# A recurrent step in which r, n and z of each half of the outputs become products of their own, in another order

## The chip, the cores and the metric

One core of one Trainium2 chip runs the whole program in one launch. The metric is device time in microseconds (us), the median of several runs. TensorE (PE; its weight loads are shown apart as PEld), VectorE (DVE), ScalarE (ACT), GpSimd (POOL) and the DMA queue of SyncE (SP) run side by side and meet at semaphores.

## The reference, cut to what matters

Four residual layers over x (4 batches, 512 time steps, 512 features): an attention layer, a recurrent cell (GRU), and two short convolutions over time. The change is in the recurrent cell alone. It goes through 512 steps, each of which needs the state of the one before:

```python
def cell(h, x):
    gi = x @ W_ih + b_ih
    gh = h @ W_hh + b_hh
    i_r, i_z, i_n = jnp.split(gi, 3, axis=-1)
    h_r, h_z, h_n = jnp.split(gh, 3, axis=-1)
    r = jax.nn.sigmoid(i_r + h_r)
    z = jax.nn.sigmoid(i_z + h_z)
    n = jnp.tanh(i_n + r * h_n)
    h_new = (1.0 - z) * n + z * h
    return (h_new, h_new)
```

## The kernel before, in words

The attention layer takes the first 570 us. After it comes the recurrent part, which is nearly three quarters of the time, with the convolutions on GpSimd beside it.

**The state.** h (4 batches, 512 features) lies transposed: features on the partitions, in four blocks k of 128; `h_of` picks a half (two of the four blocks). A step makes h new half by half. Half 0 is blocks 0 and 1, half 1 is blocks 2 and 3 (the columns of W_hh are regrouped so that each half is 64 of the 128 columns of every group G). So the products over k = 0, 1 need half 0 of h, and those over k = 2, 3 need half 1.

**TensorE.** h is the stationary operand (128 partitions by 4 columns) and W_hh streams past it. One `products` call makes, for two blocks k, four products with one column group G of the array each, so that 4 of them stand side by side. Everything is float32, and the profile shows two LDWEIGHTS and two MATMULs for each product. `begin` (line 1248) does the r and n columns together (128 columns wide) for both halves of the outputs with the first half of h; `end` (line 1258) then does r and n of output half 0 with the second half of h, z of output half 0 (64 columns wide, all four k), r and n of output half 1, and z of output half 1. Between `end` and the next `begin` a `part` (line 1286) is put in the first 448 steps: a piece of the input products (x @ W_ih) of later steps, some 0.3 us of TensorE work. The last 64 steps have none. The loop over the first 448 steps is a hardware loop whose body is four steps long, the loop over the last 64 has a body of two.

**ScalarE.** It first writes the input side (`seed_rn`, `seed_z`) into the PSUM banks, onto which the products are then added. In a step it does: sigmoid of r (`reset`, line 1199), the seeding of r and n for the next step (line 1174), sigmoid of z (`update`, line 1205), tanh (`new`, line 1210), for half 0 and then for half 1; then the two z seeds (line 1178) and the copy of the input side of n (`bring`, line 1171).

**VectorE.** It works in strict order. `turn_rn` transposes r and n of a half from PSUM (two instructions of line 1069), `turn_z` does z (line 1075), `scan_n` forms i_n + r * h_n as a scan (line 1082), `scan_h` forms the new h of the half as a scan (line 1087) and releases TensorE with `s_h`. Its order in a step is turn_rn(0), turn_z(0), scan_n(0), turn_rn(1), scan_h(0), turn_z(1), scan_n(1), scan_h(1), and the sum into the output sequence (line 1100). In some steps one of `seed_n`, `take_rz` and `take_n` follows, which carry the results of `part` out of PSUM or prepare a bank for them.

An instruction that waits for two semaphores is built as a waiting instruction of its own for one of them, with the other held on the instruction itself.

## Time and profile before

| | us |
|---|---|
| median of 3 runs | 2117.09 (2116.19 to 2117.44) |
| span of the profiled execution | 2113.7 |
| what the median has over that span | 3.4 |
| attention and set-up, up to the first recurrent product | 572.4 |
| TensorE busy | 2071.9 (98%) |
| VectorE busy | 1354.9 (64%) |
| ScalarE busy | 1239.1 (59%) |
| GpSimd busy | 638.0 (30%) |

The times list no time of its own for the profiled execution; it is its span of 2113.7 us and the 3.4 us that lie around it. Busy time of TensorE is a union of overlapping matmuls whose ends are modelled, so 98% does not say that TensorE decides the length of a step. The granted TensorE clock is full in nearly every slice. What one step is made of is read from the timeline: the order of start times on the three engines, with the durations and the idle times that it prints.

### The profile page before, as it was taken

The page shows a single profiled execution, that of the slowest core. Times are in us where ns is not written, and L with a number is a line of the kernel's source. Part 1 is how long each engine was busy: PE and PEld are TensorE (multiplying, and loading weights), DVE is VectorE, ACT ScalarE, POOL GpSimd, SP SyncE. Part 2 cuts the span into 40 slices and gives each one's busy share as a digit, 9 for nine tenths or more (in the row PEclk, how much of TensorE's full clock was granted, in tenths as well). Part 3 has the DMA queues.
Part 4 walks back from the last instruction along what each step waited for, and adds up shares of the span by engine and source line. Part 5 has one row for each costly group of instructions (what it writes and reads, how often), then busy time and mean ns, then how long its engine had stood idle before and what let it go on. Part 6 is the DMA issues. An engine that isn't in the chain of part 4 may idle for free.

```text
span 2113.7 us, 181503 instructions
## 1 busy us (share of the span) xinstructions
PE 2071.9 (98%) x77848; PEld 1578.9 (75%) x77848; DVE 1354.9 (64%) x6162; ACT 1239.1 (59%) x5995; POOL 638.0 (30%) x1015
## 2 busy tenths in 40 slices
PE   8999999999999999999999999999999999999998
PEld 2222222222499999999999999999999999998887
DVE  4344445444367777777777777777777777776676
ACT  3445544443266666666666666666666666666665
POOL 0355547444112222222222222222222222222222
PEclk9999999999999999999999999999999999999999
DMA  6000000011222222221222222222121212210001
GB/s 259 1 1 1 1 1 1 1 60 31 49 54 53 52 55 52 52 55 49 69 59 55 52 53 53 56 58 66 50 58 50 58 48 60 67 30 11 5 8 20
DMA packets 218082, 96.04 MB, mean 45 GB/s; under 512 B 170216, under 2 KB 213480, under 8 KB 217320
## 3 DMA queue, kind: packets, MB, share of 16 engines
q1 hardware_dynamic: 217032, 92.00, 16.8%
q10 hardware_dynamic: 928, 2.65, 0.3%
q8 instruction: 47, 0.77, 0.2%
q14 instruction: 75, 0.61, 0.1%
HBM read 26.30 MB, written 12.58 MB: 18 GB/s over the span
## 4 chain that ended last, share of the span: by engine, by line
PE 70%; DVE 2%; issue 0%; DMA 0%; ACT 0%; SPq 0%; DVEq 0%
PE ps L1241 64%; PE ps L1274 4%; PE ps L1282 2%; DVE arena L1069 1%; DVE arena L1087 0%; DMA arena<-arena 0%; DVE arena L965 0%; DVE arena L1075 0%; DVE arena L1082 0%; DVE arena L968 0%; ACT arena L1210 0%; SPq L994 0%; DVE arena L1158 0%; DVE seq L1163 0%; DVE seq L1100 0%
## 5 line engine op out<-in xcount | busy, mean ns | idle before, releaser
L1241 PE MATMUL ps<-whh,arena 128*4 128x128 f32 (+1 forms) x65568 | 1451.4, 246 | 13.8 <-issue 1.6
L1241 PEld LDWEIGHTS ps<-whh,arena 128*4 128x4 f32 x65568 | 1293.6, 87 | 112.2 <-DVE arena L1087 25.8
L1069 DVE STREAM_TRANSPOSE arena<-ps 128x64 f32<-128x64 f32 x2048 | 446.4, 284 | 256.1 <-PE ps L1241 237.0
L1199 ACT ACTIVATE arena<-arena 128x8 f32<-128x8 f32 x1024 | 216.1, 211 | 543.4 <-DVE arena L1069 480.1
L455 DVE TENSOR_REDUCE top<-ps 128x2 f32<-128x1024 f32 x128 | 150.8, 1220 | 244.0 <-PE ps L722 244.0
L1174 ACT ACTIVATE ps<-arena 128x128 f32<-128x128 f32 x1026 | 288.9, 282 | 0.5 <-PEq L212 0.4
L1087 DVE TENSOR_TENSOR_SCAN arena<-arena 128x24 f32<-128x24 f32 x1024 | 192.1, 188 | 145.1 <-ACT arena L1210 145.1
L1075 DVE STREAM_TRANSPOSE arena<-ps 128x64 f32<-128x64 f32 x1024 | 257.5, 251 | 9.0 <-PE ps L1241 3.3
L361 ACT ACTIVATE arena<-ps 128x1024 f32<-128x1024 f32 x128 | 124.1, 1021 | 212.7 <-PE ps L798 212.6
L610 PE MATMUL ps<-arena 128*32 128x512 f32 x2048 | 242.7, 595 | 2.7 <-ACT arena L383 2.7
L965 POOL TENSOR_TENSOR arena<-tap,arena 128x128 f32<-128x128 f32 x252 | 102.0, 415 | 430.0 <-DVE seq L1100 430.0
L1210 ACT ACTIVATE arena<-arena 128x16 f32<-128x16 f32 x1024 | 222.4, 217 | 2.0 <-DVE arena L1082 2.0
L1205 ACT ACTIVATE arena<-arena 128x8 f32<-128x8 f32 x1024 | 218.9, 214 | 3.5 <-DVE arena L1075 3.2
L1082 DVE TENSOR_TENSOR_SCAN arena<-arena 128x16 f32<-128x16 f32 x1024 | 196.3, 192 | 2.3 <-DVE arena L1075 2.2
L968 POOL TENSOR_TENSOR arena<-arena 128x128 f32<-128x128 f32 x252 | 112.6, 457 | 261.5 <-DVE seq L1100 261.5
L1178 ACT ACTIVATE ps<-arena 128x64 f32<-128x64 f32 x1026 | 181.9, 209 | 0.1
L610 PEld LDWEIGHTS ps<-arena 128*32 128x32 f32 x2048 | 61.4, 110 | 158.6 <-issue 156.9
L965 POOL TENSOR_TENSOR arena<-tap,seq 128x128 f32<-128x128 f32 x252 | 101.9, 415 | 203.2 <-DVE seq L1100 203.2
L1274 PE MATMUL ps<-arena 128*32 128x114 f32 (+1 forms) x4480 | 150.4, 242 | 2.0 <-DMA arena<-arena 2.0
L273 POOL TENSOR_TENSOR arena<-arena 128x2048 f32<-128x2048 f32 x16 | 72.8, 4551 | 212.3 <-ACT arena L361 212.3
L1100 DVE TENSOR_TENSOR seq<-seq,arena 128x16 f32<-128x16 f32 x512 | 98.5, 192 | 17.8
L1171 ACT ACTIVATE arena<-arena 128x16 f32 (+1 forms) x513 | 109.8, 214 | 0.0
(99 smaller groups left out, 1268.0 us busy)
## 6 DMA issues: line engine op xcount, KB each, us to landing
arena<-arena SPq DMA_DIRECT2D x216, 114.0 KB, 2.2
arena<-arena SPq DMA_DIRECT2D x112, 128.0 KB
arena<-seq SPq DMA_DIRECT2D x224, 55.0 KB
arena<-gi_d SPq DMA_DIRECT2D x248, 32.0 KB
gi_d<-arena SPq DMA_DIRECT2D x96, 57.0 KB
out<-seq SPq DMA_DIRECT2D x14, 256.0 KB
seq<-in_x SPq DMA_DIRECT2D x3, 1024.0 KB, 15.6
whh<-in_w_hh SPq DMA_DIRECT2D x1, 3072.0 KB, 21.1
```

The lines of the kernel that those rows point to most:

```text
L610: last = e.matmul(dst[rows], w[:, rows], v, start=start, stop=stop)
L965: return e.tensor_tensor(conv_part(k, held), along(tap[:, k]), src[:, :, bass.ds(t + k, NB)], ALU.mult)
L1069: e.transpose(trn[:, h, q].rearrange("p (i c s) -> p c i s", c=2, s=2)[:, :, :, 0], bank[RN[h]][:, 64 * q:64 * q + 64].rearrange("p (c i) ...
L1075: e.transpose(trz[:, h].rearrange("p (i c) -> p c i", c=2), bank[RZ[h]][:, 0:64].rearrange("p (c i) -> p c i", c=2)).then_inc(st["s_tr"], 1)
L1082: e.tensor_tensor_scan(pre[:, h], r_d0[:, h], trn[:, h, 1, 0:2 * NH], 0.0, ALU.mult, ALU.add).then_inc(st["s_pre"], 1)
L1087: e.tensor_tensor_scan(hb[:, 1 - u, h, 0:HS], z_d0[:, h], hb[:, u, h, 1:HS + 1], 0.0, ALU.mult, ALU.add).then_inc(st["s_h"], 1)
L1174: e.activation(bank[RN[h]][:, 0:P].rearrange("p (q n) -> p q n", q=2), at(19456 + SLOT * s + 64 * h, 512).rearrange("p (q w) -> p q w", q= ...
L1199: e.activation(r_d0[:, h].rearrange("p (i s) -> p i s", s=2)[:, :, 1], trn[:, h, 0, 0:2 * NH].rearrange("p (i s) -> p i s", s=2)[:, :, 0], ...
L1205: e.activation(z_d0[:, h].rearrange("p (i s) -> p i s", s=3)[:, :, 2], trz[:, h, 0:NH], ACT.Sigmoid)
L1210: e.activation(hb[:, u, h, 1:HS + 1].rearrange("p (i s) -> p i s", s=3)[:, :, 0:3:2], pre[:, h].rearrange("p (i s) -> p i s", s=2)[:, :, 1 ...
L1241: last = e.matmul(bank[dst[h]][32 * G:32 * G + B, 0:n], hv, wv[:, k, gates, G, 64 * h:64 * h + 64], start=False, stop=k2 == 1 and k == C - ...
L1274: last = e.matmul(bank[FA][rows, columns], a_fixed[:, k, rows], a_moving[:, k, columns], start=k == 0, stop=k == C - 1, skip_group_check=True)
```

## The change

Each of r, n and z of each half gets its own region in PSUM and, but for one case, its own products (64 columns wide). r1 and z0 lie side by side in one bank and are made together, 128 columns wide, in `begin`. There is a semaphore for every completed piece, VectorE transposes every piece by itself, and the order of all three engines is rewritten. `scan_h` now waits for the sigmoid of z by a semaphore of its own (`s_zs`) beside that of tanh. The instructions that serve `part` (`gate_op`) go from the end of VectorE's step to a place ahead of `scan_h(1)`.

```diff
-        RN, RZ, FA, FN = (0, 1), (2, 3), 4, 5
+        FA, FN = 4, 5
+        gate_r = (bank[0][:, 0:64], bank[1][:, 0:64])
+        gate_n = (bank[6][:, 0:64], bank[2][:, 0:64])
+        gate_z = (bank[1][:, 64:128], bank[3][:, 0:64])
...
                     def scan_n(h):
-                        e.wait_ge(st["s_tr"], n_at[h])
                         e.wait_ge(st["s_sig"], half[h])
+                        e.wait_ge(st["s_tn"], half[h])
...
                     def scan_h(h):
+                        e.wait_ge(st["s_zs"], half[h])
                         e.wait_ge(st["s_tanh"], half[h])
...
-                    turn_rn(0)
+                    turn_r(0)
+                    turn_n(0)
+                    scan_n(0)
                     turn_z(0)
-                    scan_n(0)
-                    turn_rn(1)
+                    turn_r(1)
+                    turn_n(1)
                     scan_h(0)
+                    scan_n(1)
                     turn_z(1)
-                    scan_n(1)
+                    gate_op()
                     scan_h(1)
...
                         reset(0)
-                        e.wait_ge(st["s_tr"], turned[1])
-                        seed_rn(0, s)
+                        seed_r(0, s)
+                        new(0)
                         update(0)
-                        new(0)
                         reset(1)
-                        e.wait_ge(st["s_tr"], turned[4])
-                        seed_rn(1, s)
+                        e.wait_ge(st["s_tn"], half[0])
+                        seed_n(0, s)
+                        seed_z(0, s)
+                        seed_r(1, s)
+                        new(1)
                         update(1)
-                        new(1)
-                        seed_z(0, s)
+                        bring(following)
+                        e.wait_ge(st["s_tn"], half[1])
+                        seed_n(1, s)
                         seed_z(1, s)
-                        bring(following)
...
                     e.wait_ge(st["s_h"], half[0])
-                    e.wait_ge(st["s_seed_rn"], half[0])
-                    products(u, RN, rn, 0, 0)
-                    e.wait_ge(st["s_seed_rn"], half[1])
-                    products(u, RN, rn, 1, 0)
+                    e.wait_ge(st["s_seed_r"], half[0])
+                    products(u, gate_r[0], "r0", 0, False)
+                    e.wait_ge(st["s_seed_n"], half[0])
+                    products(u, gate_n[0], "n0", 0, False)
+                    e.wait_ge(st["s_seed_r"], half[1])
+                    e.wait_ge(st["s_seed_z"], half[0])
+                    products(u, bank[1][:, 0:128], "r1 z0", 0, False)
...
                     e.wait_ge(st["s_h"], half[1])
-                    products(u, RN, rn, 0, 1).then_inc(st["s_rn"], 1)
-                    e.wait_ge(st["s_seed_z"], half[0])
-                    products(u, RZ, z, 0, 0)
-                    products(u, RZ, z, 0, 1).then_inc(st["s_z"], 1)
-                    products(u, RN, rn, 1, 1).then_inc(st["s_rn"], 1)
+                    products(u, gate_r[0], "r0", 1, True).then_inc(st["s_r0"], 1)
+                    products(u, gate_n[0], "n0", 1, True).then_inc(st["s_n"], 1)
+                    products(u, gate_r[1], "r1", 1, True)
+                    products(u, gate_z[0], "z0", 1, True).then_inc(st["s_rz"], 1)
+                    e.wait_ge(st["s_seed_n"], half[1])
+                    products(u, gate_n[1], "n1", 0, False)
+                    products(u, gate_n[1], "n1", 1, True).then_inc(st["s_n"], 1)
                     e.wait_ge(st["s_seed_z"], half[1])
-                    products(u, RZ, z, 1, 0)
-                    products(u, RZ, z, 1, 1).then_inc(st["s_z"], 1)
+                    products(u, gate_z[1], "z1", 0, False)
+                    products(u, gate_z[1], "z1", 1, True).then_inc(st["s_z1"], 1)
```

The second step of the four-step loop body on TensorE, from the wait for h to the last product of the step. Before (line 1241 is `products`; 4x128 and 4x64 are products 128 and 64 columns wide; a row without a wait belongs to the row above it):

```order
L1241 MATMUL ps<-whh,arena 4x128 [waits s_seed_rn,s_h]
L1241 MATMUL ps<-whh,arena 4x128 x7
L1255 REGISTER_ALU
L1241 MATMUL ps<-whh,arena 4x128 [waits s_seed_rn]
L1241 MATMUL ps<-whh,arena 4x128 x7
L1241 MATMUL ps<-whh,arena 4x128 [waits s_h]
L1241 MATMUL ps<-whh,arena 4x128 x7
L1241 MATMUL ps<-whh,arena 4x64 [waits s_seed_z]
L1241 MATMUL ps<-whh,arena 4x64 x15
L1241 MATMUL ps<-whh,arena 4x128 x8
L1241 MATMUL ps<-whh,arena 4x64 [waits s_seed_z]
L1241 MATMUL ps<-whh,arena 4x64 x15
```

And now (line 1263 is `products`):

```order
L1263 MATMUL ps<-whh,arena 4x64 [waits s_seed_r,s_h]
L1263 MATMUL ps<-whh,arena 4x64 x7
L1263 MATMUL ps<-whh,arena 4x64 [waits s_seed_n]
L1263 MATMUL ps<-whh,arena 4x64 x7
L1279 REGISTER_ALU
L1263 MATMUL ps<-whh,arena 4x128 [waits s_seed_z,s_seed_r]
L1263 MATMUL ps<-whh,arena 4x128 x7
L1263 MATMUL ps<-whh,arena 4x64 [waits s_h]
L1263 MATMUL ps<-whh,arena 4x64 x31
L1263 MATMUL ps<-whh,arena 4x64 [waits s_seed_n]
L1263 MATMUL ps<-whh,arena 4x64 x15
```

The wait for the second half of h (`s_h` alone) stood 16 products into the step and now stands 24 into it. Behind it there were 48 products, and now there are 64: r0, n0, r1 and z0 (8 each, in the rows of 1 and 31), n1 (16) and z1 (16 more, in the rows that would follow). A step had 64 products, 32 of them 128 columns wide; it now has 88, 8 of them 128 columns wide.

The same step on VectorE, one in which `take_rz` (line 1112) is due. Before (1069: r and n are transposed; 1075: z; 1082: `scan_n`; 1087: `scan_h`; the program names the scans SCALAR_TENSOR_TENSOR):

```order
L1069 STREAM_TRANSPOSE arena<-ps 128x2x32 [waits s_rn]
L1069 STREAM_TRANSPOSE arena<-ps 128x2x32
L1075 STREAM_TRANSPOSE arena<-ps 128x2x32 [waits s_z]
L1082 SCALAR_TENSOR_TENSOR arena<-arena 128x16 [waits s_sig,s_tr]
L1069 STREAM_TRANSPOSE arena<-ps 128x2x32 [waits s_rn]
L1069 STREAM_TRANSPOSE arena<-ps 128x2x32
L1087 SCALAR_TENSOR_TENSOR arena<-arena 128x24 [waits s_tanh]
L1075 STREAM_TRANSPOSE arena<-ps 128x2x32 [waits s_z]
L1082 SCALAR_TENSOR_TENSOR arena<-arena 128x16 [waits s_sig,s_tr]
L1087 SCALAR_TENSOR_TENSOR arena<-arena 128x24 [waits s_tanh]
L1100 TENSOR_TENSOR seq<-seq,arena 128x16 [waits s_h]
L1112 TENSOR_TENSOR arena<-ps,arena 128x114 [waits s_kept1,s_rzpart]
```

And now (1068: all transposes; 1085: `scan_n`; 1091: `scan_h`; 1119: `take_rz`; of two waits the first named stands in an instruction of its own):

```order
L1068 STREAM_TRANSPOSE arena<-ps 128x2x32 [waits s_r0]
L1068 STREAM_TRANSPOSE arena<-ps 128x2x32 [waits s_n]
L1085 SCALAR_TENSOR_TENSOR arena<-arena 128x16 [waits s_tn,s_sig]
L1068 STREAM_TRANSPOSE arena<-ps 128x2x32 [waits s_rz] x2
L1068 STREAM_TRANSPOSE arena<-ps 128x2x32 [waits s_n]
L1091 SCALAR_TENSOR_TENSOR arena<-arena 128x24 [waits s_tanh,s_zs]
L1085 SCALAR_TENSOR_TENSOR arena<-arena 128x16 [waits s_tn,s_sig]
L1068 STREAM_TRANSPOSE arena<-ps 128x2x32 [waits s_z1]
L1119 TENSOR_TENSOR arena<-ps,arena 128x114 [waits s_kept1,s_rzpart]
L1091 SCALAR_TENSOR_TENSOR arena<-arena 128x24 [waits s_tanh,s_zs]
L1107 TENSOR_TENSOR seq<-seq,arena 128x16 [waits s_h]
```

Ahead of the first `scan_h` stood the transposes of r and n of half 1, and they still do; n of half 1 is now complete 48 products after the wait for the second half of h, where r and n of half 1 were 32 after it. Both `scan_n` moved ahead of the transpose of z that stood before them, and `take_rz` moved ahead of the last `scan_h`.

## Rows read from the trace of the kernel before

**Rows 1.** The page: busy us, share of the span, instructions of each engine.
```profile
PE 2071.9 (98%) x77848; PEld 1578.9 (75%) x77848; DVE 1354.9 (64%) x6162; ACT 1239.1 (59%) x5995; POOL 638.0 (30%) x1015
```

**Rows 2.** Timeline, steps with a part: start us, duration us, engine, line, count, idle before.
```profile
1502.47 2.83 PE L1241 MATMUL ps<-whh,arena 128*4 128x128 f32 x128
...
1504.04 0.44 DVE L1069 STREAM_TRANSPOSE arena<-ps 128x64 f32<-128x64 f32 x2 [0.53 <-PE ps L1241]
...
1504.38 0.21 ACT L1199 ACTIVATE arena<-arena 128x8 f32<-128x8 f32 x1 [0.93 <-DVE arena L1069]
1504.48 0.25 DVE L1075 STREAM_TRANSPOSE arena<-ps 128x64 f32<-128x64 f32 x1
...
1504.69 0.19 DVE L1082 TENSOR_TENSOR_SCAN arena<-arena 128x16 f32<-128x16 f32 x1
1504.77 0.21 ACT L1205 ACTIVATE arena<-arena 128x8 f32<-128x8 f32 x1
1504.92 0.22 ACT L1210 ACTIVATE arena<-arena 128x16 f32<-128x16 f32 x1
1504.92 0.44 DVE L1069 STREAM_TRANSPOSE arena<-ps 128x64 f32<-128x64 f32 x2
...
1505.12 0.38 PE L1274 MATMUL ps<-arena 128*32 128x114 f32 x8
...
1505.23 0.17 DVE L1087 TENSOR_TENSOR_SCAN arena<-arena 128x24 f32<-128x24 f32 x1
...
1505.45 2.83 PE L1241 MATMUL ps<-whh,arena 128*4 128x128 f32 x128
...
1506.05 0.21 DVE L1087 TENSOR_TENSOR_SCAN arena<-arena 128x24 f32<-128x24 f32 x1 [0.28 <-ACT arena L1210]
...
1506.29 0.19 DVE L1100 TENSOR_TENSOR seq<-seq,arena 128x16 f32<-128x16 f32 x1
1506.39 0.27 DVE L1112 TENSOR_TENSOR arena<-ps,arena 128x114 f32<-128x114 f32 x1
```

**Rows 3.** Timeline, TensorE alone, 28 steps later.
```profile
1585.72 1.50 PE L1241 MATMUL ps<-whh,arena 128*4 128x128 f32 x48
```

**Rows 4.** Timeline, a step without a part, and the next one's first ScalarE instruction.
```profile
2050.13 0.21 ACT L1199 ACTIVATE arena<-arena 128x8 f32<-128x8 f32 x1 [0.93 <-DVE arena L1069]
...
2050.98 0.17 DVE L1087 TENSOR_TENSOR_SCAN arena<-arena 128x24 f32<-128x24 f32 x1
...
2051.20 2.09 PEld L1241 LDWEIGHTS ps<-whh,arena 128*4 128x4 f32 x96 [0.33 <-DVE arena L1087]
...
2053.10 0.21 ACT L1199 ACTIVATE arena<-arena 128x8 f32<-128x8 f32 x1 [0.93 <-DVE arena L1069]
```

**Rows 5.** Waits, 1920 to 2100 us: us in total, times, longest.
```profile
PEld ps L1241 <- DVE arena L1087: 20.5, 61, 0.7
```

**Rows 6.** Chain in order of time, 1502.6 to 1505.6 us: start us, us, what.
```profile
1502.62 2.68 PE ps L1241 x128
1505.30 0.20 PE ps L1274 x8
1505.49 0.10 PE ps L1282 x8
```

**Rows 7.** Timeline of TensorE in the loop's first pass.
```profile
585.43 0.23 PE L1241 MATMUL ps<-whh,arena 128*4 128x64 f32 x3 [0.46 <-issue]
...
585.82 2.52 PE L1241 MATMUL ps<-whh,arena 128*4 128x128 f32 x105
589.53 0.46 PE L1241 MATMUL ps<-whh,arena 128*4 128x64 f32 x20 [1.19 <-issue]
```

**Rows 8.** DMA queues, 570 to 600 us: packets, MB, share of 16 engines.
```profile
q8 instruction: 5, 0.08, 1.3%
```

**Rows 9.** DMA queues, 600 to 1910 us: the only one that carried instructions.
```profile
q14 instruction: 58, 0.48, 0.1%
```

**Rows 10.** DMA queues, 1910 to 2100 us.
```profile
q8 instruction: 2, 0.03, 0.1%
```

More of the change, by code:

```diff
@@ L1056, in _, with step @@
             def _(e):
-                def step(t, u):
+                def step(t, u, gate_op):
                     def count(v):
@@ L1131, in _, with gate_ops @@
                 seed_n(0)
-                for q in range(BODIES):
-                    for v in range(4):
-                        step(4 * q + v, v % 2)
-                        if v == 0 and q and q % 2 == 0:
-                            seed_n(q // 2)
-                        if v == 2:
-                            take_rz(q)
-                        if v == 3 and q % 2 == 1:
-                            take_n(q // 2)
-                for t in range(4 * BODIES, T):
-                    step(t, t % 2)
+                def gate_ops(t):
+                    q, v = divmod(t, 4)
+                    if q >= BODIES:
+                        return
+                    if v == 0 and q and q % 2 == 0:
+                        seed_n(q // 2)
+                    if v == 2:
+                        take_rz(q)
+                    if v == 3 and q % 2 == 1:
+                        take_n(q // 2)
+                for t in range(T):
+                    step(t, t % 2, lambda: gate_ops(t))
                 t, done = T - NB, s_end
@@ L1171, in bring, with seed, seed_r, seed_n @@
                     e.activation(n_in, gi_n[:, :, bass.ds(t, 1)].rearrange("p (h i) a -> p h (i a)", h=2), ACT.Copy)
[L1173 to L1175 removed]
+                def seed(gate, part, h, s):
+                    first = P * part + 64 * h
+                    return e.activation(gate[h], ring[:, s, first:first + 64], ACT.Copy)
+                def seed_r(h, s):
+                    seed(gate_r, 0, h, s).then_inc(st["s_seed_r"], 1)
                 def seed_z(h, s):
[L1178 to L1179 removed]
+                    seed(gate_z, 1, h, s).then_inc(st["s_seed_z"], 1)
+                def seed_n(h, s):
+                    seed(gate_n, 2, h, s).then_inc(st["s_seed_n"], 1)
                 e.wait_ge(s_ring[0], 16 * NG)
@@ L1183, in _ @@
                 for h in range(2):
-                    seed_rn(h, 0)
-                for h in range(2):
+                    seed_r(h, 0)
+                    seed_n(h, 0)
                     seed_z(h, 0)
@@ L1193, in _ @@
                         half = (e.snap(2 * t + 1), e.snap(2 * t + 2))
-                        turned = [e.snap(6 * t + i) for i in range(1, 7)]
                         following = e.snap(t + 1)
                         def reset(h):
-                            e.wait_ge(st["s_tr"], turned[3 * h])
+                            e.wait_ge(st["s_tr"], half[h])
                             e.activation(r_d0[:, h].rearrange("p (i s) -> p i s", s=2)[:, :, 1],
@@ L1232, in _, with weights, products @@
                 wv = whh[:].rearrange("p c (q G n) -> p c q G n", q=3, G=NG)
-                rn, z = slice(0, 3, 2), slice(1, 2)
-                def products(u, dst, gates, h, k2):
-                    n = len(range(3)[gates]) * 64
+                def weights(k, G, parts):
+                    if parts == "r1 z0":
+                        first = P * G + 64
+                        return whh[:, k, first:first + 2 * (D - 64)].rearrange("p (q n) -> p q n", q=2)[:, :, 0:64]
+                    gate, h = "rzn".index(parts[0]), int(parts[1])
+                    return wv[:, k, gate, G, 64 * h:64 * h + 64]
+                def products(u, dst, parts, k2, stop):
                     for k in (2 * k2, 2 * k2 + 1):
@@ L1240, in products @@
                         for G in range(NG):
-                            last = e.matmul(bank[dst[h]][32 * G:32 * G + B, 0:n], hv, wv[:, k, gates, G, 64 * h:64 * h + 64],
-                                            start=False, stop=k2 == 1 and k == C - 1, skip_group_check=True)
+                            last = e.matmul(dst[32 * G:32 * G + B], hv, weights(k, G, parts),
+                                            start=False, stop=stop and k % 2 == 1, skip_group_check=True)
                     return last
```

36 lines of the change are left out of this document (15 added, 21 removed).

## The prediction

> **What bounds the kernel now.** I read the page first. TensorE is busy for 98% of the span [rows 1], which looks like a TensorE-bound kernel. That is a trap here, so the next view is the timeline of one recurrent step. The first weight load of `begin` starts with TensorE's products at 1502.47, the next at 1505.45 [rows 2], and 28 steps after 1502.47 at 1585.72 [rows 3]: 83.25 / 28 = 2.973 us a step. In a step without a `part` the first sigmoid comes at 2050.13 and again at 2053.10 [rows 4], which is 2.97 as well, though TensorE now idles 0.33 us until `scan_h` lets it go on [rows 4]. This is so in all of the last steps (20.5 us in 61 waits, [rows 5]). A step that has 0.29 us less TensorE work and is as long is not set by TensorE. It is set by a loop of dependences, and the parts fill its hole.
>
> The loop, with E as the first product of `end`. `begin` is 16 products, 128 wide, 0.88 us, so E = 1502.47 + 0.88 = 1503.35. r and n of half 0 take 0.44; their transpose starts at 1504.04 [rows 2], E + 0.69, which is 0.25 after the last product's slot. z0 takes 0.45 more and its transpose is at E + 1.13, rn1 ends at E + 1.32 and its transpose starts at 1504.92, E + 1.57: always 0.25. Tanh of half 0 is running by then (1504.92), but `scan_h(0)` stands behind the two transposes and starts at 1505.23, E + 1.88. TensorE is let go 0.22 later (1505.45), and 0.88 of `begin` leads to the next E: 1.88 + 0.22 + 0.88 = 2.98, the step. The second half is as tight: `scan_h(1)` starts at 1506.05 [rows 2], and 0.28 later the next `end` begins.
>
> **TensorE's own work.** Step less idle is 2.973 - 0.33 = 2.64 us [rows 4], for 64 products, which are 128 MATMULs. They go in fours. The chain gives 0.20 us for 8 MATMULs of 114 columns and 0.10 for 8 of 55 [rows 6]; so four cost 0.10 and 0.05, about 0.85 ns a column and 2 ns on top. That makes 0.109 for 128 columns and 0.056 for 64, and 16 x (0.109 + 0.056) = 2.64. The change turns 12 wide fours into 24 narrow ones: 24 x 0.056 - 12 x 0.109 = +0.03 (with the 2 ns unrounded), so 2.67 us. `part` is 0.29 to 0.30 (0.20 + 0.10, [rows 6]). TensorE alone would now need 2.965 us in a step with a part, 0.008 less than the step of before.
>
> At this place the Trainium skill speaks against the change (TensorE: Matmul & The Clock Gate, "Back-to-back issue gap"): narrow matmuls do not come closer than about 25 ns start to start. By that rule 176 MATMULs would be 4.4 us a step. The trace disagrees already: 128 of them would be 3.2 us and fit in 2.68 [rows 6], 21 ns on average over both widths. It gives no rival.
>
> **The new loops.** With slots of 0.056, r0 ends at E + 0.22, n0 at 0.45, r1 and z0 at 0.89, n1 at 1.34, z1 at 1.79. Each transpose can start 0.25 later. The links, from [rows 2]: transpose to its sigmoid 0.34 from rest and 0.29 behind other work; sigmoid to a scan 0.31 where the wait stands in an instruction of its own (1504.38 to 1504.69), 0.24 where it is held by the instruction itself, as tanh to `scan_h(1)` has it; scan to tanh 0.23; one transpose to the next about 0.15 to 0.17.
>
> First half: turn_r at 0.47, reset at 0.81, `scan_n(0)` at 1.06 (the sigmoid is now the wait held by the instruction; n's transpose allows 1.07), tanh at 1.30. turn_z(0) could start at 1.14 and waits for the scan: 1.21. Its sigmoid is at 1.50, and frees `scan_h(0)` at 1.74. VectorE is there at 1.59 (turn_n of half 1) + 0.17 = 1.76. So `scan_h(0)` starts at E + 1.77, where it was at 1.88, and TensorE may go on at 1.99. With a part it is busy until 1.79 + 0.29 = 2.08 anyway. This loop is hidden in the first 448 steps.
>
> Second half: turn_n(1) at 1.59 ends at 1.90; `scan_n(1)` follows 0.10 later at 2.00, tanh at 2.23. turn_z(1) could start at 2.04 and gets VectorE at 2.07 to 2.14, its sigmoid comes at 2.36 to 2.43, is done 0.21 later, and `scan_h(1)` starts at 2.60 to 2.67. With the 0.27 from there to the products of `end`, the next E is at 2.87 to 2.94. With a part TensorE is the later one (2.965). Without one the chain is: I take the middle, 2.905.
>
> `gate_op` in front of `scan_h(1)` waits for `part`, whose first pieces are done some 0.2 behind z1; `take_rz` would run from about E + 2.25 for 0.27 us (duration from [rows 2]) while VectorE waits for the sigmoid of z1. `take_n` waits for the whole part, starts at about 2.33, and is out of the way by 2.6. Cost 0, hidden by that wait; without the cover each would add up to 0.1 us in a quarter or an eighth of the steps. The seeds are now six small ones. Seed r1, the latest that `begin` needs, is written by E + 2.3, and TensorE wants it at 2.42 with a part and at 2.33 without. The second waiting instruction of `scan_h` is met long before: line 1112 has one too and starts 0.10 behind line 1100 [rows 2], so a met wait costs nothing.
>
> **Code loading.** The product loop on TensorE grows. Before, a pass of four steps is 4 x 256 instructions, 128 for the parts and some 20 others: 1170. After, it is 4 x 352 + 128 + 22 = 1560. The trace shows the code arriving in blocks of 16 KB (0.08 MB in 5, [rows 8]) during the first pass only: none in the 1300 us after it [rows 9]. TensorE stops at 585.43 and 589.53 for no reason but "issue" [rows 7]; between the stops lie 126 MATMULs (those of the first and second row and four small groups), so with the weight loads a block is about 256 instructions, and a first-time block costs 4.10 us where 256 instructions run in 3.0. Counting back in 256s, the loop starts nearly at a block's start, and 589.53 is its fourth boundary. From there the pass of before has 145 instructions left, 1.6 us, ending at 591.1. The new loop starts 32 instructions later in its block (`begin` ahead of it has 8 more products), and 1560 + 32 is six blocks and 56: two more boundaries, 589.53 + 2 x 4.10 + 0.5 = 598.2. That is +7.1 us once. The loop over the last 64 steps brings 2 new blocks [rows 10] at almost no stall now, because 256 instructions last a whole step. At 352 a step each block outruns the work by about 2 us, less some tenths: one or two stalls, +2.5.
>
> **Sum**, against the profiled span of 2113.7 us: 444 steps x (2.965 - 2.973) = -3.6; 62 x (2.905 - 2.973) = -4.2; first pass +7.1; second loop +2.5. Together +1.8, a span of 2115.5. With the 3.4 us that the median has over the span: 2119 us.
>
> **Rivals.** (a) The loading is hidden or cheaper, or was part of another wait (the first pass also waits for DMAs): 2118.9 - 9.6 = 2109.3. For it: the first steps are full of other waits. Against it: two stops exactly one block apart [rows 7]. (b) Slower: `scan_h` waits on two engines' results, and if a wait in an instruction of its own costs 0.06 (the 0.31 against 0.24 above) even when it is met, or the sigmoid of z1 gets behind the seeds on ScalarE, the second half's loop goes from 2.94 through 2.965 to about 3.00. Its place is turn_n(1), `scan_h(0)`, `scan_n(1)`, turn_z(1); it decides as soon as it is 0.03 longer than I have it. 444 x 0.035 + 62 x 0.095 = +21: 2140 us. For it: five VectorE operations in a row, each priced from another neighbourhood. Against it: line 1112. With twice that slip (3.03) it would be 2155.
>
> (c) The longer loop does not stay loaded. By the Trainium skill (Runtime: NRT & Kernel Launch, "Instruction fetch mechanics") TensorE holds 128 KiB, 2048 instructions, in 16 KiB blocks: eight, and the new loop touches seven and has the next one fetched ahead, so it would just fit. No run here shows the limit; the loop of before, which stays loaded [rows 9], touches five blocks. In this kernel, without a figure of the page: if it doesn't fit, each of 112 passes takes 6.1 x 4.10 = 25 us and not 11.9, +1470 us, about 3590. I can't exclude it.
>
> **Chances.** Forecast 0.47, (a) 0.25, (b) 0.24, (c) 0.04. Within 0.2% (4.2 us, about what a measurement can tell from no change) is 2112.9 to 2121.3. Of the forecast's part some falls above it, since its narrow range is 2113 to 2124; (a) is mostly faster, (b) and (c) slower. Faster 0.25, same 0.40, slower 0.35. The range is 2108 to 2136: it holds (a) and half of (b).
>
> **What would show it.** Right: steps with a part at 2.965 with TensorE never waiting for `scan_h`, steps without one at 2.87 to 2.94 with idle time before `end` and no longer before `begin`, `scan_h(0)` at E + 1.77, stops of "issue" about 4.1 us apart up to 598, and no block of TensorE code between 610 and 1900. Wrong: TensorE waiting for line 1091 in steps with a part (b), a first pass that ends near 591 (a), fours of narrow MATMULs further apart than 0.056, or code blocks throughout (c).

## The result, and the profile after

The changed kernel takes 2135.7 us (median of 4 runs, 2134.68 to 2138.47), the kernel before 2116.64 on the same chip (4 runs, 2115.37 to 2117.44). The ratio is 1.0097, with a 95% interval from 1.0083 to 1.0111: 0.97% slower. The forecast was 2119, no change. The profiled execution has a span of 2132.9 us, 19.2 more than the one of before, and those 19.2 us are what the traces have to account for. With before there is now a time for the profiled execution itself, 2115.37 us: 1.7 us lie around its span of 2113.7, and 1.8 around that of after. The rest of the 3.4 us that I added was the spread between executions.

The page of the kernel after, which answers to [rows 1]:

```profile
PE 2088.6 (98%) x102440; PEld 1630.1 (76%) x102440; DVE 1384.8 (65%) x6162; ACT 1245.1 (58%) x7021; POOL 638.3 (30%) x1015
```

TensorE's busy time grew by 16.7 us, VectorE's by 29.9 (with as many instructions), ScalarE's by 6.0. None of these says where the time went. To find the place I took the start of the sum into the output sequence (line 1107, before 1100) in each of the 512 steps, from both traces, and subtracted:

| stretch (us) | before | after | difference | predicted |
|---|---|---|---|---|
| up to the first sum, and from there four steps (the first pass) | 576.2 + 17.8 | 578.3 + 22.0 | +6.3 | +7.1 |
| steps 4 to 448, with a part | 1323.8 | 1335.1 | +11.3 | -3.6 |
| steps 448 to 450 (the second loop begins) | 6.13 | 8.70 | +2.6 | +2.5 |
| steps 450 to 511, without a part | 181.7 | 180.7 | -1.0 | -4.2 |

Of the 17.4 us that the forecast misses, 14.9 are in the second line and 3.2 in the fourth. The step in the second line took 2.981 us before and takes 3.007 (means), but not every one: by place in the four-step loop body of TensorE the medians are 2.986, 2.954, 2.962 and **3.081**. The last of the four holds the end of one pass and the start of the next. Before, all four are 2.973 or 2.974.

Timeline of the kernel after, the weight loads of TensorE over one pass (start us, duration us, engine, line, count, idle before):

```profile
1910.62 2.72 PEld L1263 LDWEIGHTS ps<-whh,arena 128*4 128x4 f32 x176
...
1913.67 2.67 PEld L1263 LDWEIGHTS ps<-whh,arena 128*4 128x4 f32 x176
...
1916.61 2.69 PEld L1263 LDWEIGHTS ps<-whh,arena 128*4 128x4 f32 x176
...
1919.51 0.86 PEld L1263 LDWEIGHTS ps<-whh,arena 128*4 128x4 f32 x48
1920.56 1.79 PEld L1263 LDWEIGHTS ps<-whh,arena 128*4 128x4 f32 x128 [0.20 <-DVE arena L1091]
```

Three times `begin` and `end` run through in one piece of 176. The fourth time they are 48 and 128, with 0.20 us of nothing between, just where the loop goes back. The view names `scan_h` (line 1091) as what TensorE waited for. The view of waits says the same of the whole stretch (620 to 1900 us: total us, times, longest), where there are 107 passes:

```profile
PEld ps L1263 <- DVE arena L1091: 26.9, 124, 0.4
```

Taken at its word, this line is my rival (b). But the view names the last thing that was released, and not when. The same back edge as in the section on it below, first VectorE's `scan_h(1)`, then the first weight load of the next pass, in after (timeline, 1509.5 to 1512.5 us):

```profile
1510.94 0.21 DVE L1091 TENSOR_TENSOR_SCAN arena<-arena 128x24 f32<-128x24 f32 x1 [0.28 <-ACT arena L1220]
...
1511.38 1.18 PEld L1263 LDWEIGHTS ps<-whh,arena 128*4 128x4 f32 x84 [0.21 <-DVE arena L1091]
```

The scan ends at 1511.15 and the load starts 0.23 us later. Where a load does wait for the scan, it follows faster: in before the scan ends at 1509.23 (1509.019 + 0.208) and the load starts at 1509.28. Over the 107 back edges between 620 and 1900 us, the load starts 0.054 us after the end of `scan_h(1)` in before (median, and within 0.06 in 105 of them), and 0.22 us after it in after (within 0.06 in 3). In after, then, VectorE was done, and something on TensorE's own side held the load.

TensorE's products say the same from the other side. From the first product of `begin` to the first MATMUL of the next `part`, they take 2.643 us in before, with a back edge between them or without. In after they take 2.670 without one and 2.776 with one (medians). From the part's first MATMUL to the next `begin` it is 0.330 in before, where `begin` waits for h, and 0.295 in after, where it doesn't. 2.670 + 0.295 is the 2.965 of the forecast; the 0.106 of the back edge is what it lacks. The experiments below change TensorE and VectorE one at a time.

The last 64 steps, which answer to [rows 4]:

```profile
2051.45 0.53 DVE L1068 STREAM_TRANSPOSE arena<-ps 128x64 f32<-128x64 f32 x2 [0.31 <-PE ps L1263]
...
2052.07 0.27 DVE L1085 TENSOR_TENSOR_SCAN arena<-arena 128x16 f32<-128x16 f32 x1
...
2052.77 0.21 DVE L1091 TENSOR_TENSOR_SCAN arena<-arena 128x24 f32<-128x24 f32 x1
...
2053.03 1.25 PEld L1263 LDWEIGHTS ps<-whh,arena 128*4 128x4 f32 x70 [0.28 <-DVE arena L1091]
```

With E = 2050.97, the first product of `end`, `scan_h(0)` starts at E + 1.80 (forecast 1.77) and TensorE goes on at E + 2.06 (forecast 1.99). So `scan_n(0)` is 0.04 late, because its transpose of n is the later input, and the scan to TensorE takes 0.26 where I had 0.22. TensorE still idles ahead of `begin`, and not ahead of `end` as I wrote. The back edge is felt here too: between 1925 and 2100 us the first load behind one starts 0.14 us after the end of `scan_h(1)` (median of 28; in before 0.05), and the steps that hold one take 2.969 us where the others take 2.938 (medians).

The first pass, which answers to [rows 7], TensorE:

```profile
577.04 0.45 PE L1263 MATMUL ps<-whh,arena 128*4 128x64 f32 x17 [2.30 <-issue]
...
584.96 2.38 PE L1263 MATMUL ps<-whh,arena 128*4 128x64 f32 x127 [1.41 <-issue]
588.60 0.46 PE L1263 MATMUL ps<-whh,arena 128*4 128x64 f32 x19 [1.26 <-issue]
...
592.92 1.44 PE L1263 MATMUL ps<-whh,arena 128*4 128x64 f32 x89 [2.08 <-issue]
596.60 2.80 PE L1263 MATMUL ps<-whh,arena 128*4 128x64 f32 x154 [1.64 <-issue]
```

The stops now go on to 596.6, where they ended at 589.53. The DMA queues carry 50 blocks of TensorE's instructions in the whole program. Between 570 and 602 us there are six of them, a seventh comes at 622 us, and then there is none up to 1910 us: the seven blocks of the loop stay loaded.

```profile
q8 instruction: 50, 0.82, 0.2%
```

### The profile page after: what moved, and what is told of

Its sections match the earlier page's. It is cut to its first block, busy times and chain, and to the rows that moved or that the text cites. A ratio compares the mean times of both kernels' runs of the same rounds, so it can differ in the third digit from the quotient of the medians.

```text
span 2132.9 us, 230034 instructions
## 1 busy us (share of the span) xinstructions
PE 2088.6 (98%) x102440; PEld 1630.1 (76%) x102440; DVE 1384.8 (65%) x6162; ACT 1245.1 (58%) x7021; POOL 638.3 (30%) x1015
## 4 chain that ended last, share of the span: by engine, by line
PE 94%; DVE 3%; ACT 1%; issue 1%; ACTq 0%; DMA 0%; DVEq 0%; SPq 0%
PE ps L1263 62%; PE ps L613 14%; PE ps L1301 4%; PE ps L798 3%; PE ps L725 3%; PE ps L816 3%; PE ps L1309 2%; DVE arena L1068 1%; PE ps L828 1%; PE ps L801 1%; DVE arena L1085 1%; DVE arena L1091 0%; ACT arena L1225 0%; ACT arena L1220 0%; ACT arena L364 0%
## 5 line engine op out<-in xcount | busy, mean ns | idle before, releaser
L1263 PE MATMUL ps<-whh,arena 128*4 128x64 f32 (+1 forms) x90160 | 1484.4, 224 | 18.4 <-issue 11.5
L1263 PEld LDWEIGHTS ps<-whh,arena 128*4 128x4 f32 x90160 | 1363.4, 87 | 82.7 <-DVE arena L1091 45.8
L1068 DVE STREAM_TRANSPOSE arena<-ps 128x64 f32<-128x64 f32 x3072 | 719.1, 271 | 219.9 <-PE ps L1263 217.8
L1186 ACT ACTIVATE ps<-arena 128x64 f32<-128x64 f32 x3078 | 544.6, 208 | 0.4 <-DMA arena<-arena 0.4
L1091 DVE TENSOR_TENSOR_SCAN arena<-arena 128x24 f32<-128x24 f32 x1024 | 203.3, 199 | 105.3 <-ACT arena L1220 85.8
L1085 DVE TENSOR_TENSOR_SCAN arena<-arena 128x16 f32<-128x16 f32 x1024 | 214.7, 210 | 75.9 <-ACT arena L1214 2.3
L613 PEld LDWEIGHTS ps<-arena 128*32 128x32 f32 x2048 | 61.7, 110 | 159.1 <-issue 157.7
L1301 PEld LDWEIGHTS ps<-arena 128*32 128x32 f32 x4480 | 95.0, 110 | 0.1
L1309 PE MATMUL ps<-arena 128*32 128x55 f32 (+1 forms) x2688 | 85.5, 227 | 0.0
```

Source lines behind the costliest of these rows:

```text
L613: last = e.matmul(dst[rows], w[:, rows], v, start=start, stop=stop)
L1068: return e.transpose(dst, src.rearrange("p (c i) -> p c i", c=2))
L1085: e.tensor_tensor_scan(pre[:, h], r_d0[:, h], trn[:, h, 1, 0:2 * NH], 0.0, ALU.mult, ALU.add).then_inc(st["s_pre"], 1)
L1091: e.tensor_tensor_scan(hb[:, 1 - u, h, 0:HS], z_d0[:, h], hb[:, u, h, 1:HS + 1], 0.0, ALU.mult, ALU.add).then_inc(st["s_h"], 1)
L1186: return e.activation(gate[h], ring[:, s, first:first + 64], ACT.Copy)
L1263: last = e.matmul(dst[32 * G:32 * G + B], hv, weights(k, G, parts), start=False, stop=stop and k % 2 == 1, skip_group_check=True)
```

## The experiments

Two stand ahead of all: is it TensorE's own instruction stream at the loop's end, or VectorE, which reaches `scan_h(1)` late? Each ratio is to the kernel before on the same chip. The experiments ran on three chips, on which before takes 2115.4 us (`e1` to `e4`), 2116.4 (`e5`, `e6`, `e8`, `e9`) and 2115.5 (`e10`, `e11`), where it took 2116.6 beside after; so times of different groups are compared by what they have over their own before.

### One wait fewer on TensorE

In `begin` of the changed kernel two semaphores are waited for ahead of the product of r1 and z0, one of them in an instruction of its own with a register operation ahead of it. Here the two seeds count on one semaphore.

```diff
-                    e.wait_ge(st["s_seed_r"], half[1])
-                    e.wait_ge(st["s_seed_z"], half[0])
+                    e.wait_ge(st["s_seed_rz"], half[0])
                     products(u, bank[1][:, 0:128], "r1 z0", 0, False)
```

> The changed kernel, in which TensorE reaches the wide product of begin (r1 and z0) with one wait against a register that is there already, where it had a register operation and two waits; the seeds count on other semaphores for it, nothing else moves. Theory A: the changed kernel loses time at the back edge of TensorE's loop. There the sequencer needs 0.47 us from the last product of a pass to the first of the next, and has only some four fours of MATMULs in hand; the two instructions ahead of the wide product eat 0.17 us of that, so 0.11 us stands open in every pass of four steps. Without them the gap closes: 111 x 0.11 = 12 us less, 2122 to 2125 us, and the step that begins a pass takes 2.97 us and not 3.08. Theory B: the 0.11 us are VectorE's, which does take_n ahead of scan_h(1) at the end of a pass, as the profile's releaser (line 1091) says: then nothing changes, 2134 to 2137 us.

Measured: 2128.16 us (2126.92 to 2129.88), ratio to before 1.0058 [1.0044 to 1.0071], against 1.0097 [1.0083 to 1.0111] for after: 12.8 us over before and not 19.1. The traces have steps 4 to 448 shorter by 7.8 us and the start of the second loop by 1.8, and the stretch up to step 4 longer by 3.5, of which 2.4 lie ahead of the first recurrent product, in the attention layer. The four medians are 2.986, 2.955, 2.961 and 2.996: only the interval over the back edge moved, by 0.085. With nothing changed on VectorE, the same line of waits reads

```profile
PEld ps L1268 <- DVE arena L1091: 8.7, 38, 0.4
```

so most of the waits "for VectorE" went with one wait of TensorE's. They shrank rather than vanished: the view lists idle times over 0.15 us alone, and the weight loads' idle time at the back edges went from 0.21 to 0.15 us (medians), 22.2 to 15.6 us in all. The array's products over a back edge went from 2.776 to 2.705. The time is 3 us above theory A's range and 6 below theory B's: the back edge still costs 2.996 - 2.965 = 0.03 a pass, 3.4 us in 111 of them, which A had at nothing.

### The part's VectorE work last again

```diff
                     turn_z(1)
-                    gate_op()
                     scan_h(1)
...
+                    gate_op()
```

> The changed kernel with the instructions that serve the parts (gate_op) back at the end of VectorE's step, behind the sum into the output, as they stood before. Theory A (back edge of TensorE's loop): no change, 2134 to 2138 us, and the first step of a pass stays at 3.08 us. Theory B (take_n holds scan_h(1) back at the end of a pass): about 10 us less, 2124 to 2127 us.

Measured: 2135.63 us (2134.74 to 2139.09), and the waits are 27.2 us in 124, medians 2.987, 2.945, 2.961, 3.081. Only one median moved, from 2.954 to 2.945, and the one over the back edge did not. So `gate_op` ahead of `scan_h(1)` is not what the back edge waits for, and my "cost 0" for this move holds.

### The kernel before with narrow products

r and n of each half are products of their own, in the order of before: 96 products a step, and a `begin` that ends with narrow ones.

```diff
-                            last = e.matmul(bank[dst[h]][32 * G:32 * G + B, 0:n], hv, wv[:, k, gates, G, 64 * h:64 * h + 64],
+                            last = e.matmul(bank[dst[h]][32 * G:32 * G + B, 64 * i:64 * i + 64], hv, wv[:, k, gate, G, 64 * h:64 * h + 64],
```

> The kernel before, with its order, its waits and its transposes, but r and n of a half as products of their own, 64 columns wide: 96 products a step and not 64. It does the narrowing alone. From the loop of dependences: rn0 and rn1 in end and both in begin get 0.01 us longer each, 3.01 us a step and not 2.973, +20 us. First pass and second loop load 0.5 times more code: about +10 us. By theory A the back edge is open too, since four narrow fours are only 0.22 us in hand: up to 0.25 us in each of 112 passes and in 32 of the second loop, +20 to +35 us. Sum by theory A 2165 to 2182 us; if the back edge costs nothing here, 2145 to 2150 us. If the narrowing were free and only the new order cost the time: 2117 to 2120 us.

Measured: 2185.3 us (2184.54 to 2187.2), ratio 1.0331 [1.0315 to 1.0347], 3 us above theory A's range and 35 above the next. The medians are 3.014, 3.012, 3.014 and 3.262. The narrow products cost the 0.04 us a step that the fours predict, and the back edge another 0.25 a pass, here with the kernel's old waits. Here too the last 64 steps, which go back every two steps, are 3.143 in the mean where they had been 2.978. In this kernel the waits view puts the idle time at the back edge down to "issue", since `scan_h(1)` had ended 0.33 us before the load (median). It names VectorE in 11 waits with 2.9 us; the row of the back edge is

```profile
PEld ps L1245 <- issue: 28.2, 111, 0.4
```

### What happens at the back edge

Rows of the trace of after for one back edge, with the instructions that the views don't count (start us; fours of MATMULs by their first, and the time since the last four; some fours are left out at the top):

```
1510.617 REGISTER L1279          1510.619 four of 64   +0.056
1510.714 WAIT L1280              1510.731 four of 64   +0.056
                                 1510.843 four of 128  +0.056
1510.911 REGISTER L1336          1510.952 four of 128  +0.109
1511.008 BRANCH L1336            1511.061 four of 128  +0.109
                                 1511.170 four of 128  +0.109
1511.274 REGISTER L1336
1511.383 first LDWEIGHTS         1511.390 four of 64   +0.220
```

On the left is what TensorE's instruction stream does, on the right what the array does. The stream runs ahead of the array. From the register operation at the loop's end to the first weight load of the next pass it takes 1511.383 - 1510.911 = 0.47 us in which it issues no product. At 1510.911 the array had work until 1511.170 + 0.109 = 1511.279 in hand, so it stands still for 0.11: the four comes 0.220 after the last where 0.109 was due. The kernel before has the same three instructions, and there it is 0.51 us from 1508.771 to the load at 1509.282. That includes the wait for h, since `scan_h(1)` ended at 1509.227. The array had wide fours in hand past that, and the next one came after 0.109. The changed kernel spoils the lead twice: narrow products bring half the array time for the same number of instructions, and the register operation and the wait ahead of r1 and z0 take some 0.1 us each out of the stream just before. The second is what `e1_one_wait` took away, and what the first four of a pass comes late went from 0.11 to 0.04 (medians). The first is what `e3_before_narrow` added, and there the four comes 0.25 late. What is left in `e1_one_wait`, 0.04, no run took away. The Trainium skill (Advanced Engine Details and Errata, "Control Flow Timing") gives a compare-and-branch about 108 ns. The trace shows 208 ns for that instruction and 0.47 us for the whole turn, and here the measurement decides.

### A loop body of eight steps

```diff
-                with e.Fori(0, BODIES) as it:
-                    for v in range(4):
+                with e.Fori(0, BODIES // 2) as it:
+                    for v in range(8):
```

> The changed kernel with a loop body of eight steps on TensorE, 56 passes and not 112: about 3090 instructions, 12.1 blocks of code. If a body of any length stays loaded: 56 back edges less (-6 us), six more first-time blocks at 2 us each (+12 us), about 2142 us. If the code has to be fetched in every pass because it doesn't fit: 12.1 x 4.1 = 50 us a pass and not 24, 56 x 26 = +1450 us, about 3590 us, with some 700 code blocks in the trace.

Measured: 3606.49 us in the one run. Half as many back edges, and a disaster:

```profile
q8 instruction: 771, 12.63, 1.5%
```

721 blocks more than the kernel after had, in 56 passes: each pass of some 3100 instructions has all its blocks, 13 or so, fetched again. The extra time is (3604.7 - 2132.9) / 721 = 2.0 us a block. The granted clock is 0.91 from 620 to 1900 us here and 1.00 in after, so some of the 2.0 can be the clock's; how much, no run shows. This is rival (c), with its mechanism and size, at a length that the change does not reach.

### r1 and z0 in one product in `end` too

```diff
-                    products(u, gate_r[1], "r1", 1, True)
-                    products(u, gate_z[0], "z0", 1, True).then_inc(st["s_rz"], 1)
+                    products(u, bank[1][:, 0:128], "r1 z0", 1, True).then_inc(st["s_rz"], 1)
```

This stands on top of `e1_one_wait`.

> The kernel with one wait ahead of the wide product, and besides r1 and z0 made in one 128-wide product in `end` too (80 products a step for 88). Theory A (TensorE is the bound of the steps with a part, its loop's back edge and the first-time loading of code come on top, as measured): two wide fours for four narrow ones twice in a step save 4 x 0.056 x 2 - 2 x 0.109 x 2 = 0.011 us a step, -5 us over 448; 32 instructions fewer a step are half a block less in the first pass, -2, and up to -1 in the second loop. 2119 to 2122 us. Theory B (after the one wait something on VectorE or ScalarE holds the steps, not TensorE): -2 or -3 for loading alone, 2125 to 2127; and if r1's later completion sits in the chain, 2130 or more.

Measured: 2120.93 us (2118.9 to 2122.54, 9 runs), ratio 1.0021 [1.0011 to 1.0031]. The stretch from step 4 to 448 lost 4.9 us against `e1_one_wait` (0.011 a step, as worked out), and the first pass 4, of which I had expected 2; the start of the second loop got 1.4 longer. Theory A holds: TensorE's own time is the bound of these steps.

### The second loop four steps long

```diff
-                with e.Fori(2 * BODIES, T // 2) as it:
-                    for v in range(2):
+                with e.Fori(BODIES, T // 4) as it:
+                    for v in range(4):
```

> The changed kernel, with the loop over the last 64 steps written four steps long instead of two: 2 x 352 = 704 more instructions, 2.75 blocks, to be loaded once. Theory A (a block met for the first time costs TensorE about 2 us over the work it holds): +5.5, and -0.6 for half as many back edges: 2139 to 2142 us. Theory B (what follows step 448 is a wait of another kind, and loading is hidden): -0.6 or nothing, 2134.5 to 2136.

Measured: 2137.75 us (2136.28 to 2141.04), some 2 more than after, between the two theories. The trace tells them apart. The queues carry 5 blocks of TensorE's code after 1910 us where it was 3, and the steps from 448 to 460 are 3.6 us longer: 1.8 a block. After that they are 0.6 shorter, the back edges saved. So a first-time block costs about what theory A says, and my count of 2.75 blocks was too high. How many boundaries a stretch meets also depends on where the blocks happen to end: steps 448 to 450 take 6.13 us in before, 6.93 in `e1_one_wait` and 8.70 in after.

### Where VectorE's blocks of code end

One thing remained. Besides the regular intervals, steps in both kernels are now and then 0.06 to 0.35 us too long, without a pattern in the loop: 18 steps with 3.4 us in all before, 39 with 7.8 us after (steps 8 to 444, above the median of their place; in after 2.9 us of that come back in steps that are shorter than their median, in before nothing). VectorE's program has no loop there, all 512 steps are written out, and the queue [rows 9] fetches blocks of 8 KB, most of them 24 us apart in after, the time in which VectorE gets through 128 instructions. I counted VectorE's instructions along the stream, those that are never busy too: of the pauses over 0.1 us in after, 38 fall at the same number, 66 modulo 128, with 8.9 us. (The number depends on where one begins to count; by the trace's own records, counted from zero, it is 63.) So two kernels were made from `e5_wide_in_end` with the same spare instructions on VectorE (an increment of a semaphore that nobody waits for), one in eight steps, so that 128 instructions are exactly eight steps. They differ only in how many stand at the start (and ahead of the last 64 steps).

```diff
+                for _ in range(7):
+                    spare()
...
+                    if v == 3 and q % 2 == 0:
+                        spare()
```

> The kernel of e5_wide_in_end with spare semaphore instructions on VectorE, one in eight steps and a few at the start, so that its written-out stream is 128 instructions in eight steps and the point 66 into each 128 falls on the first transpose of a step, ahead of which VectorE idles. Theory A (the irregular stops of 0.06 to 0.35 us are VectorE changing to its next block of code, and cost only where they fall into its chain): 4 to 8 us less than e5_wide_in_end, about 2114 to 2116. Theory B (they come from something else, or TensorE's own time hides them): the same as e5_wide_in_end within 1.5 us.

With 11 spares at the start:

> As e8_dve_blocks_slack, with the point 66 into each 128 instructions put on the transpose of z of half 1, ahead of the last `scan_h` of a step. Theory A: a stop of up to 0.3 us in the chain of the second half, 55 times, where e5_wide_in_end has some of them: 4 to 10 us more than e5_wide_in_end, and 10 or more above e8_dve_blocks_slack. Theory B: the same as both within 1.5 us.

Measured: 2114.52 us (2112.31 to 2116.42, 11 runs) with the boundary in VectorE's idle time, ratio 0.9993 [0.9984 to 1.0002], and 2128.49 us (2127.4 to 2131.4), ratio 1.0062 [1.0048 to 1.0076], with the boundary in the chain. The same instructions with four spares more at the start make 14 us; `e5_wide_in_end` lies between them, 6.4 above the one and 7.6 below the other. In the first, one step in 436 is too long by more than 0.06 us, and the mean from step 8 to 444 is 2.964 us. In the second the stop can be seen where it was put, and steps 4 to 448 are 13.8 us longer than in the first. VectorE in its trace:

```profile
1510.16 0.19 DVE L1085 TENSOR_TENSOR_SCAN arena<-arena 128x16 f32<-128x16 f32 x1
1510.54 0.25 DVE L1068 STREAM_TRANSPOSE arena<-ps 128x64 f32<-128x64 f32 x1 [0.19 <-issue]
1511.07 0.21 DVE L1091 TENSOR_TENSOR_SCAN arena<-arena 128x24 f32<-128x24 f32 x1 [0.28 <-ACT arena L1235]
```

The transpose of z of half 1 starts 0.38 after the scan ahead of it, where the first kernel has 0.11 (1511.20 to 1511.31):

```profile
1511.20 0.19 DVE L1085 TENSOR_TENSOR_SCAN arena<-arena 128x16 f32<-128x16 f32 x1
1511.31 0.23 DVE L1068 STREAM_TRANSPOSE arena<-ps 128x64 f32<-128x64 f32 x1
```

The view of waits of the second has it 53 times from 620 to 1900 us, once in eight steps:

```profile
DVE arena L1068 <- issue: 10.4, 53, 0.2
```

### The same spares in the kernel before and in the kernel after

In the kernel before:

```diff
+                        spare(3 if v == 3 and q % 2 == 0 else 2)
```

> The kernel before, with spare semaphore instructions on VectorE after each step (two a step, one more in every eighth, three in the last 64, seven at the start), so that its stream is 128 instructions in eight steps and the point 66 into each 128 falls where VectorE idles ahead of the first transpose of a step. Theory A (VectorE's code blocks cost where they fall into the chain; before had 18 such stops with 3.4 us, and e8_dve_blocks_slack gained 6.4): 3 to 4 us less than before, a ratio of 0.998 to 0.9986, about 2112.5 to 2113.5. Rival (the two spare instructions a step are not hidden): 0.05 us a step more, +20 us; or no change, if in before the stops come from elsewhere.

Measured: 2113.07 us (2111.11 to 2115.42, 11 runs) against 2115.45 of before on the same chip (15 runs), ratio 0.999 [0.9981 to 0.9999]. From step 4 to 448 the trace is 3.2 us shorter, and the four medians stay at 2.973 to 2.975, so the spares themselves cost nothing. By the time it gained 2.4 us, a little less than the 3 to 4 I had expected. It is the only kernel here whose interval lies below 1, by little; `e8_dve_blocks_slack` can't be told from before, nor the two from each other.

The changed kernel with the spares and nothing else:

> The changed kernel with the spare VectorE instructions of e8_dve_blocks_slack and nothing else, so TensorE's two waits and its narrow products of r1 and z0 stay. If VectorE's code blocks and TensorE's back edge are costs that add: 5 to 7 us less than the changed kernel, 2128.5 to 2131. If the gap at TensorE's back edge is itself a consequence of VectorE's stops: 2121 or less. If TensorE's own time hides the stops here: 2135 to 2136.

Measured: 2132.95 us (2130.83 to 2135.98), ratio 1.0084 [1.0071 to 1.0098]: 17.5 us over before, where after had 19.1. The two intervals overlap, so the times alone don't show a gain, and I had expected 5 to 7 us. What shows it is the trace: steps 4 to 448 lost 5.1 us, and their medians are 2.983, 2.952, 2.960 and 3.086. The back edge is untouched by VectorE's stops: the products over it take 2.776 us as before. So the two causes are separate, and neither explains the other away.

With both kernels freed of VectorE's stops the change can be read cleanly: 1320.6 us before, 1330.0 after from step 4 to 448, +9.4. The rest of the +11.3, about 2 us, is that the stops fell worse for the changed kernel.

## Why the prediction was wrong, step by step

**The bound of the steps with a part: right.** I said that the loop through `scan_h(0)` gives way to TensorE, at 2.965 us a step. The three intervals without a back edge are 2.983, 2.952 and 2.960 in `e11_after_blocks_slack`, 2.965 in the mean, and TensorE's own record has 2.670 for the products (forecast 2.67) and 0.295 for the part (0.29 to 0.30). The fours of narrow MATMULs are 0.056 apart and the wide ones 0.109.

**The failed step is "TensorE alone would now need 2.965 us in a step with a part".** It counts products and leaves out the loop that they stand in. I had priced the back edge at nothing without saying so: in the trace of before it was invisible, since TensorE had both a queue of wide products in hand and a wait for h at the same place (the load 0.054 us behind the end of `scan_h(1)`). Making TensorE the bound took the wait, narrow products and the extra wait took the lead. It costs 3.086 - 2.965 = 0.12 us in each of 111 passes, +13.4, and 13.4 - 3.6 = 9.8 stands beside the 9.4 measured. (By the products alone it is 0.106 a pass, 11.8 us.) I weighed each added wait for what it waits for ("is met long before"), and not for what the instruction itself takes from the stream of the engine that is now the bound.

**The code loading: right in kind, and in size.** From the first recurrent product to the sum of step 4 it is 21.6 us before and 28.2 after: +6.6 for +7.1. The part of it ahead of the first sum is the change's as well. From the first recurrent product to that sum it takes 3.8 us in before and in `e10_before_blocks_slack`, and 6.2 in after, which has its first stop of 2.30 us there; what else `e10_before_blocks_slack` has over before, 2.1 us, lies ahead of the first recurrent product. In the second loop it is +2.6 for +2.5, but that this term came out so well is partly luck: in `e1_one_wait` the same two steps have only 0.8 more than before. `e6_second_loop_4` bears the price of about 2 us a block out, and so does `e4_body_8` with 721 of them, as far as its lower clock allows. The Trainium skill (Runtime: NRT & Kernel Launch, "Instruction fetch mechanics") gave eight blocks of room: seven stay and thirteen don't, which agrees with it and does not fix the limit at eight.

**The last 64 steps: the size was off.** The term was -4.2 and measured -1.0. The second half came as forecast (`scan_h(1)` at E + 2.63, forecast 2.60 to 2.67), but the loop through `scan_h(0)`, which I had at 1.99 + 0.88 = 2.87, came to 2.06 + 0.89 = 2.95 and binds. I had two links a few hundredths too short, and averaged the other loop where the later one decides. The back edge has a share in this too: the steps that hold one are 0.031 longer, about 1 us in 31 of them.

**The rivals.** (b), slower through VectorE's second half, has the right sign and nearly the right time (2140) for the wrong reason: the loads at the back edge start 0.22 us after `scan_h(1)` has ended, and between back edges TensorE takes the 2.965 us of its own work. That the time lies within the range is luck: (b) stretched it that far. (a) fell with the loading. A term that was nowhere: VectorE's stops, 2 us of the difference.

**The sum, as measured:** +6.3 first pass, +9.4 TensorE (13.4 of it the back edge, -3.6 the steps), +1.9 VectorE's blocks, +2.6 second loop, -1.0 the last steps: +19.2.

## What to carry to other kernels

When a change makes an engine the bound, price its whole instruction stream, with branches, register operations and separate waits, and not only its work: what was hidden under a wait becomes time, and narrow products halve the work that a queued instruction brings. If a gap recurs with the period of a loop body, suspect the loop, whatever engine a view of waits names, and test it by changing that engine alone. And before a difference of some tenths of a per cent is put down to an edit, ask whether the edit only moved where blocks of a long written-out program end: four idle instructions more at the start moved a kernel here by 14 us.

## What the runs showed of the hardware that I had not expected

- TensorE's turn from the end of a loop body to its start takes 0.47 us in its instruction stream (median in after, `e1_one_wait` and `e3_before_narrow`; the 0.51 of before ends with a wait for VectorE), of which the compare-and-branch is 0.208. It shows as 0 (before), 0.03 (`e1_one_wait`), 0.12 (after) or 0.25 us (`e3_before_narrow`) a pass, depending on how much array time stands in the queue.
- VectorE, going through written-out code, has a stop of up to 0.35 us at one place in every 128 instructions (53 times in 1280 us in `e9_dve_blocks_chain`), and this is seen in the time only if it falls into the chain. That it is bound to the count of instructions, and not to the step, is what two kernels with a shifted stream confirmed. Why it is there stays open: in `e9_dve_blocks_chain` the queue's next fetch starts 0.68 us behind the stop (median of 53) and the one before it mostly 23 us ahead, and what the engine waits for at the stop no view shows.
- A block of 256 TensorE instructions met for the first time costs about 2 us over the work it holds (1.8 in `e6_second_loop_4`, 2.0 in `e4_body_8`, there at a clock of 0.91). A loop of seven blocks stays loaded, one of thirteen is fetched anew in each pass, and a run of 2135 us becomes one of 3606.
- An idle gap's releaser can be wrong in a whole class of cases: 26.9 us in 124 waits were put down to VectorE, 106 of them at the back edge, where its scan had ended 0.22 us earlier (median). The time between the releaser's end and the start of what it released tells: it is 0.054 us where the wait is real.
